# Attention of the second layer: transposes of shift and output in pieces over sixteen steps, means ten steps ahead, alternating row halves in the score pairs

## The reference

```python
v = _log_map(mu, x)
q = proj_h(v @ Wq.T)          # 15 clipped features and a leading one, sqrt(1 + sum sp**2 + EPS)
k = proj_h(v @ Wk.T)
vv = jnp.transpose((v @ Wv.T).reshape(B, T, h, dh), (0, 2, 1, 3))
sc = (-jnp.einsum('bhqi,bhki->bhqk', q[..., :1], k[..., :1]) + jnp.einsum('bhqc,bhkc->bhqk', q[..., 1:], k[..., 1:])) / dh ** 0.5
at = jax.nn.softmax(sc, axis=-1)
out = jnp.einsum('bhqk,bhkc->bhqc', at, vv)
```

## Time and profile before

| | us |
|---|---|
| median of 3 runs | 2615.57 (2615.17 to 2617.49) |
| the profiled execution, its own time | 2617.34 |
| span in the profile | 2615.5 |
| attention loop, first exponential to end of the last | 803.15 to about 1799.3 |
| ACT busy in that loop | 968.1 |
| PE busy in that loop | 984.9 |

### The profile page before, as it was taken

How to read it: one execution, slowest core, us unless ns; L and a number is a source line. 1 busy time by engine, 2 the same in 40 slices (tenths; PEclk the granted TensorE clock), 3 DMA queues, 4 the chain that set the end, 5 groups by cost and what they waited for, 6 DMA issues and landing times. The chain is left out here.

```text
span 2615.5 us, 41239 instructions
## 1 busy us (share of the span) xinstructions
PE 2241.7 (86%) x12824; PEld 1058.3 (40%) x12825; DVE 1267.7 (48%) x2731; ACT 1490.9 (57%) x2463; POOL 383.2 (15%) x628
## 2 busy tenths in 40 slices
PE   4995799922978999999999999999157999999993
PEld 3783555511651222222222222224124666666662
DVE  5566422254885444444444444421465444444444
ACT  2212433213766999999999999997643222222220
POOL 0030366640000000000000000000001222222220
PEclk9998899965998999999999999999678999999996
DMA  5001122253100000000000000003353444434445
GB/s 179 1 1 65 33 79 78 74 187 124 36 14 1 1 1 1 1 1 1 1 1 1 1 1 1 1 1 102 93 169 103 122 121 118 120 118 118 120 116 210
DMA packets 106610, 164.39 MB, mean 63 GB/s; under 512 B 9592, under 2 KB 82032, under 8 KB 106480
## 3 DMA queue, kind: packets, MB, share of 16 engines
q1 hardware_dynamic: 91696, 121.24, 15.1%
q0 software_dynamic: 13632, 37.24, 4.3%
q10 hardware_dynamic: 1152, 4.19, 0.4%
HBM read 123.06 MB, written 39.58 MB: 62 GB/s over the span
## 5 line engine op out<-in xcount | busy, mean ns | idle before, releaser
L1661 ACT ACTIVATE at_pexp<-at_psS 128x1024 f32<-128x1024 f32 x1024 | 968.1, 1023 | 59.9 <-PE at_psS L1561 56.9
L1675 DVE TENSOR_REDUCE at_mx<-at_psM 128x1 f32<-128x512 f32 x474 | 327.5, 691 | 478.4 <-PE at_psM L1588 478.4
L1575 PE MATMUL at_psO<-at_pexp,at_vst 128*32 128x512 f32 x4096 | 546.5, 606 | 0.1
L1561 PE MATMUL at_psS<-l1c_QT,l1c_KT 64*128 64x512 f16 x2048 | 404.3, 387 | 12.2 <-ACT at_pexp L1661 6.1
L1561 PEld LDWEIGHTS at_psS<-l1c_QT,l1c_KT 64*128 64x128 f16 x2048 | 100.7, 93 | 616.7 <-ACT at_pexp L1661 555.7
L1988 PE MATMUL ex_psH<-wide_wgu,ex_xT 128*128 x852 | 339.7, 549 | 0.1
L2032 ACT ACTIVATE ex_sg<-ex_bias 128x228 f32<-128x228 f32 x213 | 83.7, 393 | 287.9 <-DVE ex_bias L2058 287.9
L2058 DVE TENSOR_TENSOR ex_bias<-ex_psH,ex_bias 128x456 f32<-128x456 f32 x213 | 134.7, 633 | 198.5 <-PE ex_psH L1988 197.3
L1988 PEld LDWEIGHTS ex_psH<-wide_wgu,ex_xT 128*128 128x128 f32 x852 | 157.4, 191 | 138.1 <-issue 138.0
L1005 POOL DMA_INDIRECT expert_rows<-ex_y,ex_odx x142 | 140.4, 989 | 397.8 <-issue 281.4
L2011 PE MATMUL ex_psY<-wide_w2b,ex_hT 114*128 (+1 forms) x852 | 196.0, 380 | 0.7 <-DVE ex_y L2077 0.7
(11 more groups left out here) (335 smaller groups left out, 2696.0 us busy)
## 6 DMA issues: line engine op xcount, KB each, us to landing
ex_bias<-in_L_ffn_bg SPq DMA_DIRECT2D x71, 342.0 KB, 4.7
ex_bias<-in_L_ffn_b SPq DMA_DIRECT2D x71, 342.0 KB, 5.1
normed<-rt_area SPq DMA_DIRECT2D x16, 512.0 KB, 2.6
lm_y<-expert_rows SPq DMA_DIRECT2D x16, 512.0 KB
cb_y<-expert_rows SPq DMA_DIRECT2D x16, 512.0 KB, 9.6
w_raw<-in_L_ffn_w SPq DMA_DIRECT2D x24, 256.0 KB, 4.2
wide_wgu<-in_L_ffn_Wg SPq DMA_DIRECT2D x8, 684.0 KB
wide_wgu<-in_L_ffn_W SPq DMA_DIRECT2D x8, 684.0 KB
```

The lines of the kernel that those rows point to most:

```text
L1561: mm = pe.matmul(psS[:, n, hh * BANK:(hh + 1) * BANK], keys(k.KT, p)[r, kt * P:(kt + 1) * P], keys(k.QT, p)[r, c * BANK:(c + 1) * BANK], s ...
L1575: mm = pe.matmul(psO[g * VW:(g + 1) * VW, y, :], vst[:, p % 2, hh, kt, :], pexp[:, (p * ST + step) % 3 * 2 + n, hh * BANK:(hh + 1) * BANK] ...
L1661: act.activation(pexp[:, u % 6, :], psS[:, u % 2, :], ACT.Exp, scale=D ** -0.5 / (QS * QS)).then_inc(raised, 1)
L1675: dve.tensor_reduce(mx[:, n:n + 1], psM[:, :], AX.X, ALU.max).then_inc(reduced, 1)
```

## The change

It does four things, all in `attention`.

- Each `turn_shift` of 16 transposes is cut into four pieces of four, in four steps that follow each other: half 0 in steps 22 to 25, half 1 in steps 26 to 29. Each `turn_out` of four transposes is cut into four of one: y = 0 in steps 3 to 6, y = 1 in steps 8 to 11. `put_shift` and `divide` stand in the step of the last piece.
- The pieces stand ahead of `means` in their step, where the whole transposes stood behind it.
- AHEAD goes from 6 to 10: the shift of the next pair is made in step 21, and ten means of pair 1 are in the prologue, four of them behind the transposes (PE) and copies (DVE) of pair 0's shift.
- In odd steps the two matmuls of a score pair are written with row half 1 first.

```diff
-    AHEAD = 6
-    TURNS = (ST - 5, ST - 3)
+    AHEAD = 10
+    PIECES = 4
+    OUT_AT = (3, 8)
+    SHIFT_AT = (ST - AHEAD, ST - AHEAD + PIECES)
...
                     pe.wait_ge(raised, u + 1)
-                    for hh in range(2):
+                    for hh in (step % 2, 1 - step % 2):
...
-                def turn_shift(p, half):
-                    pe.wait_ge(shifted, p + 1)
+                def turn_shift(p, half, piece):
                     use = x_use["shift", p, half]
-                    if use:
-                        pe.wait_ge(x_free, use)
+                    if piece == 0:
+                        pe.wait_ge(shifted, p + 1)
+                        if use:
+                            pe.wait_ge(x_free, use)
                     view = psX[:, :].bitcast(F16)
-                    for hh in range(2):
-                        row = hh * HR + ROW
-                        for n in range(KT16 // 2):
+                    hh, first = piece // 2, piece % 2 * 4
+                    row = hh * HR + ROW
+                    for n in range(first, first + 4):
...
+                def turn_out(p, y, c):
+                    if c == 0:
+                        pe.wait_ge(o_out, 2 * p + y + 1)
+                        pe.wait_ge(x_free, x_use["out", p, y])
+                    mm = pe.transpose(psX[:, c * P:(c + 1) * P], oT[:, y, c * P:(c + 1) * P], k.ident[:, :])
...
                         scores(p, step, 1)
+                        for i in range(2):
+                            if OUT_AT[i] <= step < OUT_AT[i] + PIECES and p:
+                                turn_out(p - 1, i, step - OUT_AT[i])
+                            if SHIFT_AT[i] <= step < SHIFT_AT[i] + PIECES and p + 1 < NPAIR:
+                                turn_shift(p + 1, i, step - SHIFT_AT[i])
                         q, n = mean_at(p, step)
                         if q < NPAIR:
                             means(q, n)
-                        if step in (3, 5) and p:
-                            turn_out(p - 1, step // 4)
-                        if step in TURNS and p + 1 < NPAIR:
-                            turn_shift(p + 1, TURNS.index(step))
...
                 make_shift(0)
-                for t in range(AHEAD // 2):
+                for t in range(3):
                     first_reduce(1, t)
                 put_shift(0, 0)
                 put_shift(0, 1)
+                for t in range(3, AHEAD // 2):
+                    first_reduce(1, t)
...
-                        if step in (3, 5) and p:
-                            divide(p - 1, step // 4)
-                        if step in TURNS and p + 1 < NPAIR:
-                            put_shift(p + 1, TURNS.index(step))
+                        for i in range(2):
+                            if step == OUT_AT[i] + PIECES - 1 and p:
+                                divide(p - 1, i)
+                            if step == SHIFT_AT[i] + PIECES - 1 and p + 1 < NPAIR:
+                                put_shift(p + 1, i)
```

More of the change, by code:

```diff
@@ L1601, in first_means @@
                                   start=True, stop=True).then_inc(maxed, 1)
-                def turn_shift(p, half):
-                    pe.wait_ge(shifted, p + 1)
+                def turn_shift(p, half, piece):
                     use = x_use["shift", p, half]
-                    if use:
-                        pe.wait_ge(x_free, use)
+                    if piece == 0:
+                        pe.wait_ge(shifted, p + 1)
+                        if use:
+                            pe.wait_ge(x_free, use)
                     view = psX[:, :].bitcast(F16)
-                    for hh in range(2):
-                        row = hh * HR + ROW
-                        for n in range(KT16 // 2):
[L1612 to L1621, removed]
+                    hh, first = piece // 2, piece % 2 * 4
+                    row = hh * HR + ROW
+                    for n in range(first, first + 4):
+                        mm = pe.transpose(view[row:row + 1, n * P:(n + 1) * P],
+                                          shift[:, (half * (KT16 // 2) + n) * 2 + hh, :], k.identh[:, :])
+                    if piece == PIECES - 1:
+                        mm.then_inc(x_turned, 1)
+                def turn_out(p, y, c):
[3 more added lines that the diff above has]
+                    mm = pe.transpose(psX[:, c * P:(c + 1) * P], oT[:, y, c * P:(c + 1) * P], k.ident[:, :])
+                    if c == PIECES - 1:
+                        mm.then_inc(x_turned, 1)
                 pe.wait_ge(start, 2)
@@ L1625, in _ @@
                     first_means(0, t)
-                for t in range(AHEAD // 2):
+                for t in range(3):
                     first_means(1, t)
                 for half in range(2):
-                    turn_shift(0, half)
+                    for piece in range(PIECES):
+                        turn_shift(0, half, piece)
+                for t in range(3, AHEAD // 2):
+                    first_means(1, t)
                 pe.wait_ge(reduced, ST + AHEAD)
@@ L1650, in _ @@
                 for y in range(2):
-                    turn_out(NPAIR - 1, y)
+                    for c in range(PIECES):
+                        turn_out(NPAIR - 1, y, c)
             @block.scalar
```

## The result

The changed kernel takes 2658.4 us in the median of five runs (2657.4 to 2662.7) against 2616.0 for the kernel before: a ratio of 1.0165, 95% interval 1.0151 to 1.0179. It is slower by 42 us, where 2655 us had been forecast. Its profiled execution took 2658.65 us, with a span of 2656.7.

The account below looks back on a forecast made before the run. ACT's exponentials set the floor, 1.87 us a step, with about 0.1 us of room on PE. Longer pairs gave +37 us and the prologue +2.3, so +39: 2655 us against 2615.57, range 2645 to 2663 (chance 0.62).

Parts of the forecast that it names:

- The step as PE's sum: PE's distances of starts in a step: 2.17 us with a shift piece, 2.11 with an output piece, instead of 1.87.
- The wait for psX: At the piece of step 26, PE waits 0.9 us for DVE's copies to give psX back; bounds 0 and 1.2.
- The shift made one step ahead: The shift is made from step 21's mean; PE reaches the piece after 1.96 us, needs 2.1: 0.1 us of waiting.
- The pair: One pair of heads in the loop: 59.9 + 5.2 = 65.1 us instead of 62.43; together +37 us.
- The prologue: Four more means reduced before the loop, two DVE operations behind the second put, for which PE waits: +2.3 us.
- Alternating halves: Writing row half 1 first in odd steps' score pairs gains zero, since the half sharing the mean's rows must wait.
- Rival (c): Mean and next score pair run fully side by side, 0 instead of 0.215 us apart: 2610 or 2597 us; chance 0.06.
- (a): Row-shape switch partly hidden ahead of a mean, or psX back in time: 2642, or 2620 to 2633 us; chance 0.20.
- (b): Pieces are swallowed, each costing only its share of the columns, steps near 1.9 us: 2610 to 2622 us; chance 0.05.
- The gaps in ACT's timeline: ACT stalls of about 0.3 us in each of steps 4 to 7, 9 to 12 and 23 to 30.
- The lower clock at the loop's start: First scores run at the lower of TensorE's two clocks, perhaps a little longer after the change; counted as nothing.
- the ways in and out: On PE, 0.32 us into a transpose and 0.155 out, against 0.055 between two; weight loads said to lie open there.

Follow-up runs that it names:

- e1_gap: The changed kernel with one step between the two halves of the shift (half 1 in steps 27 to 30): 2649.5 us, ratio 1.0123 to the kernel before.
- e3_ahead10: The kernel before with the means ten steps ahead and the changed kernel's prologue, transposes still whole: 2619.7 us, ratio 1.0012.
- e2_halves: The changed kernel with row half 0 always first in the score pairs, as before: 2658.1 us, ratio 1.0156 to the kernel before.
- e4_alt: The kernel before with only the alternating row halves of the score pairs: 2615.7 us, ratio 0.9995.
- e5_weigh: The changed kernel with every piece between first score pair and weigh, DVE's puts and divisions ahead of the maximum: 2619.2 us, ratio 1.0004 to the kernel before.
- e7_two_rows: The kernel before with the 16 transposes of a shift half alternating between output rows 32 and 96: 2609.1 us, ratio 0.9967.

## Why the prediction was right

It held by its own steps, and most of its terms can be read.

- **The step as PE's sum.** 2.17 and 2.11 us were forecast for a step with a piece; 2.17 and 2.11 were measured. The way out ahead of a mean, the one distance that no row of before showed, was taken from the way out ahead of a score pair (0.155 and 0.26) and measured as 0.16 and 0.26.
- **The wait for psX.** 0.9 us forecast, 0.91 measured, at the piece of step 26, released by L1716 as named. The run e1_gap took it away; a new wait elsewhere took back a third of the gain, and 9 us were left of it.
- **The shift made one step ahead.** 0.1 us of waiting forecast; in the trace the first piece starts 1044.53 - 1044.16 = 0.37 us after its score pair instead of 0.32, 0.05 of waiting.
- **The pair.** 65.1 forecast, 65.06 measured; the loop 37 us longer forecast, 1033.9 - 996.2 = 37.7 measured.
- **The prologue.** +2.3 us forecast; from the first put to the first exponential it is 2.5 us longer, in the changed kernel and in e3_ahead10.
- **Alternating halves.** Zero forecast; e2_halves and e4_alt both show none. Rival (c), that mean and scores would run fully side by side, falls with them. The matmul in the mean's own half starts 0.2 us later in either order.
- **Rivals (a) and (b)**, cheaper or swallowed pieces, fall by the trace. In e5_weigh the same pieces became cheap when their neighbours changed. Rival (b) was also priced wrong: its own terms, 1.765 + 0.15 and 1.765 + 0.075 us a step and 1.0 us of waiting a pair, give about 2602 us and not 2610 to 2622.
- **What was off.** The gaps in ACT's timeline were said to be about 0.3 us in each such step; they are 0.17 and 0.23, since an exponential lasts 0.1 us longer than the distance to the next. The distances of starts were right. The lower clock at the loop's start was counted as nothing: pair 0 became 2.7 us longer (65.24 instead of 62.56) where 2.0 had been forecast, and the second stall there is 0.70. Of the 41.2 us by which the two spans differ, 37.7 are the loop and 2.5 the prologue, 0.5 are gained ahead of it, and the other 1.5 lie behind the loop and were not looked into. The forecast's 37.2 + 2.3 = 39.5 is thus short by 0.5 in the loop, 0.2 in the prologue and 1.0 outside both, for which it had no term.

The prediction's reason for the ways in and out is weaker than its numbers. It took from the Trainium skill (TensorE: Matmul & The Clock Gate, Part 3) that weight loads overlap running matmuls only where the row group differs, and said that the trace agrees. It does at the two ends, where the load of the next matmul is recorded only at that matmul's start. Elsewhere it does not: in a plain step of the kernel before, the mean's load starts 0.02 us after the score pair that is still running in its rows, and 0.21 ahead of the mean itself:

```profile
1031.63 0.10 PEld L1588 LDWEIGHTS at_psM<-at_ksumT,l1c_QT 64*128 64x128 f16 x1
```

Nor does the size of the load show: the way in from 64 rows is the same 0.32 us ahead of weights of 1 column (shift), 32 (`weigh`) and 128 (output). What the runs show is a price for going from work on 64 rows to work on 128 and back; what inside PE makes it is open. The forecast used the distances alone and did not hang on the reason. For the changed kernel they told enough: the same 0.32 us stands ahead of `weigh` in every step, so the place of a piece decides whether it is paid again.

## What to carry to other kernels

Ask of a small matmul what stands beside it before asking how small it is: in one place four transposes cost 0.41 us of PE, in another 0.17, and with their output rows in turn 0.07. Add up one step as distances of starts in the trace, and compare the sum with the pace of the engine that it feeds: PE's busy time, 984.9 of the loop's 996 us, doesn't tell that 0.1 us of room was left in a step, nor that it was no more. And where work is spread over more steps, follow its single buffer to the next user, for the copy that gives it back has not been cut.

## What the runs showed of the hardware

- Transposes that write one output row each (32 or 96) ran beside matmuls of the other column groups: `weigh` started 0.01 us after the first of them (e5_weigh), though its code stands behind all four.
- Sixteen such transposes with the two output rows in turn started within 0.39 us, eight and eight within 0.61 us, four on one row within 0.17 us. For otherwise equal instructions the order alone made e7_two_rows 8.6 us faster (interval 5 to 12), more than the 4 to 6 expected.
- From a score pair on 64 rows, the next matmul on 128 rows started 0.32 us later whichever it was, `weigh` or transpose; the next mean on 64 rows 0.23 us later.
- A single f32 transpose of 128 x 128 held `weigh` back for 0.26 us (e5_weigh), where one with a single output row held it back for 0.01.
